# Routed experts as 79 items over sorted tokens instead of 21 chunk pairs over all tokens

## The reference, cut to what matters

```python
HID = [256, 512, 768, 1024, 256, 512, 768, 1024]
h = x @ down_w + down_b                                  # 512 -> 256
logits = x @ router_w + router_b - COST_LAMBDA * cost
probs = jax.nn.softmax(logits, axis=-1)
topv, topi = jax.lax.top_k(probs, 2)
gate = jax.nn.softmax(topv, axis=-1)
for k in range(2):
    mask = jax.nn.one_hot(topi[..., k], 8)
    acc = 0
    for e, (w1, b1, w2, b2) in enumerate(expert_params):
        hm = h * mask[..., e:e + 1]
        acc = acc + (_gelu(_gelu(hm) @ w1 + b1) @ w2 + b2)
    out = out + acc * gate[..., k:k + 1]
out = out + 0.1 * (_gelu(_gelu(h) @ shared_w1 + shared_b1) @ shared_w2 + shared_b2)
out = out @ up_w + up_b + (_gelu(x) @ core_w + core_b)
```

## Time and profile before

| | |
|---|---|
| median of 3 runs | 3310.86 us (3310.76 to 3313.55) |
| profiled execution | 3309.52 us, its span 3307.8 us |
| PE busy | 2947.3 us, 89% of the span |
| DVE, ACT, POOL busy | 62%, 46%, 7% |
| mean granted clock of PE | 0.952 |
| stage of the mixture | 617 to 1312.5 us |

### The profile page before, as it was taken

One profiled execution on the slowest core, in us unless ns is written; L12 is line 12 of the kernel. 1 busy time (PEld: TensorE's weight loads), 2 busy tenths in 40 slices (PEclk: granted clock), 3 DMA queues, 4 the chain that ended last, 5 costly groups with the idle time before them and its releaser, 6 DMA issues. The chain is left out here.

```text
span 3307.8 us, 45608 instructions
## 1 busy us (share of the span) xinstructions
PE 2947.3 (89%) x13676; PEld 1769.8 (54%) x13676; DVE 2044.3 (62%) x3875; ACT 1530.8 (46%) x3177; POOL 242.8 (7%) x234
## 2 busy tenths in 40 slices
PE   8999978799999997998998998997898888983787
PEld 4455434336999994665655655654343343432343
DVE  5566645444665665756756856754847475756776
ACT  5445422223555552444543542644555566564454
POOL 0000030002000000101102102101000000000010
PEclk9999989898999998999999999998898989895899
DMA  3000022000000001200000000001000000004000
GB/s 121 13 13 0 13 90 89 33 21 9 12 13 11 11 10 38 109 1 14 1 1 14 1 1 13 1 1 61 2 21 2 21 2 21 2 2 153 7 19 26
DMA packets 43028, 82.10 MB, mean 25 GB/s; under 512 B 6256, under 2 KB 21376, under 8 KB 39392
## 3 DMA queue, kind: packets, MB, share of 16 engines
q1 hardware_dynamic: 39952, 71.60, 6.1%
q0 software_dynamic: 2896, 8.31, 0.8%
HBM read 55.25 MB, written 4.19 MB: 18 GB/s over the span
## 5 line engine op out<-in xcount | busy, mean ns | idle before, releaser
L1765 DVE TENSOR_REDUCE x_neg_max<-bank 128x2 f32<-128x1024 f32 x256 | 299.0, 1217 | 27.8 <-PE bank L1602 27.8
L1190 PE MATMUL bank<-a_wo,a_att_cols 128*128 128x512 f32 x512 | 226.9, 594 | 6.7 <-DVE a_att_cols L1303 3.7
L1240 ACT ACTIVATE a_probs<-bank,a_neg_max 128x128 f32<-128x128 f32 (+3 forms) x256 | 138.3, 540 | 190.2 <-DVE a_neg_max L1338 189.9
L955 DVE TENSOR_TENSOR moe_hid_low<-moe_hid,moe_hid_high 128x512 fp32r<-128x512 f32 x168 | 116.3, 692 | 177.1 <-ACT moe_hid_high L825 169.8
L116 PE MATMUL bank<-all_ident,a_probs 128*128 128x128 f32 x1216 | 197.0, 275 | 17.8 <-DMA a_probs<-all_x_tok 17.8
L116 PEld LDWEIGHTS bank<-all_ident,a_probs 128*128 128x128 f32 x1216 | 155.4, 142 | 105.7 <-issue 52.5
L1232 ACT COPY a_probs_t<-bank 128x128 f32<-128x128 f32 (+3 forms) x256 | 108.6, 424 | 194.9 <-PE bank L116 194.9
L1621 PE MATMUL bank<-x_q_cols,x_k_cols 64*128 64x512 f32 x512 | 160.8, 445 | 35.7 <-ACT x_x_rows L1691 12.7
L753 PE MATMUL bank<-moe_w_high,moe_hid_low 128*128 128x256 f32 x672 | 190.3, 283 | 0.0
L753 PE MATMUL bank<-moe_w_low,moe_hid_high 128*128 128x256 f32 x672 | 190.2, 283 | 0.0
L753 PE MATMUL bank<-moe_w_high,moe_hid_high 128*128 128x256 f32 x672 | 189.4, 282 | 0.1
(11 more groups left out here) (353 smaller groups left out, 6639.0 us busy)
## 6 DMA issues: line engine op xcount, KB each, us to landing
x_x_rows<-all_x_tok SPq DMA_DIRECT2D x8, 1024.0 KB, 6.3
moe_w<-in_L_ffn_e_w SPq DMA_DIRECT2D x40, 128.0 KB, 2.2
all_x_tok<-in_x SPq DMA_DIRECT2D x1, 4096.0 KB, 17.8
x_c_rows<-in_ctx SPq DMA_DIRECT2D x8, 512.0 KB, 4.4
moe_x_rows<-all_x_tok SPq DMA_DIRECT2D x4, 1024.0 KB, 4.7
a_probs<-all_x_tok SPq DMA_DIRECT2D x4, 1024.0 KB, 4.5
a_wqkv<-in_L_attn_Wqkv SPq DMA_DIRECT2D x1, 4096.0 KB, 20.0
a_wo<-in_L_attn_Wo SPq DMA_DIRECT2D x1, 4096.0 KB, 29.6
```

The source lines that it names most:

```text
L1190: last = pe.matmul(mm[g % 2], att_cols[:, h % HALF_HEADS, j * P:(j + 1) * P], wo[:, h, :], start=h == first, stop=h == end - 1)
L1240: act.activation(probs[:, n % SLOTS, 0:t], sc[n % 4][:, 0:t], ACT.Exp, bias=neg_max[:, n:n + 1], accum_out=row_sum[:, n:n + 1]).then_inc(s ...
L1765: dve.tensor_reduce(neg_max[:, g % 2, j, 2 * pair:2 * pair + 2], pair_banks[slot % 2], AX.X, ALU.max, negate=True) \
```

## The change

The experts' weights are packed at the start: in `self_attention_0` POOL issues 60 DMAs (`pack_experts`) that copy, for each of 20 pairs of chunks, w1, w2 and b1 of the pair side by side into `packed.items`, 128 rows of 1026 values in device memory. In `cross_attention_0` POOL also clears `packed.sorted`, 6144 rows of 256 values.

In the mixture, the shared expert is computed in the first part in plain f32 (`shared_in`, `shared_out`), and gelu(h) is transposed back to rows (`turn_hidden`). The choice runs once over all 16 tiles. From it DVE computes, with one PE matmul for ranks, for each token and choice its place in an order sorted by expert, each expert's share padded to whole tiles of 256, and for each of 79 items which tile (`which[i, 0]`) and which weight pair (`which[i, 1]`) it works on. 79 is the most that any choice needs; all 79 are always run. POOL scatters gelu(h) with 32 indirect DMAs into `packed.sorted`. In the item loop SP loads tiles and weights with the numbers from `which`, PE turns a tile (`turn_rows`), multiplies in plain f32 (`hidden`, `output`), ACT copies the tile of an item and does the gelus, DVE adds the result to the tile in `acc`. Finished tiles are stored to `packed.mixed`; POOL fetches them back per token with 32 indirect DMAs, DVE weighs them (`combine`), and up projection and norm follow as before, each batch behind its rows.

```diff
+PAIRS = [c // 2 for c in CHUNKS]
+TOKENS = 256
+SPARE = (TOP_K * B * S + EXPERTS * (TOKENS - 1)) // TOKENS
+TILES = SPARE + 1
+def pack_experts(pool, packed, a):
+    for e in range(EXPERTS):
+        for n in range(PAIRS[e]):
...
+            pool.dma_start(to[:, 0:half].rearrange("p (k n) -> p k n", k=KL), chunked(a[f"L0_ffn_e{e}_w1"][:, at])) \
+                .then_inc(packed.items_in, 16)
...
+    TURN = [SPARE] + list(range(SPARE))
+    AHEAD, SLOTS, RETURNED = 4, 3, 8
...
+            def load_item(i):
+                if i >= SLOTS:
+                    sp.wait_ge(*filled(("item", i - SLOTS)))
+                pair = sp.value_load(which[i:i + 1, 1:2], min_val=0, max_val=PAIR0[EXPERTS] - 1)
+                sp.dma_start(item[:, i % SLOTS, :], packed.items[bass.ds(pair, 1)].rearrange("o p n -> p (o n)")) \
+                  .then_inc(s.item_in[i % SLOTS], 16)
+            def load_rows(n):
+                if n >= AHEAD:
+                    sp.wait_ge(*emptied(("turn", n - AHEAD)))
...
+            def store_tile(t):
+                sp.wait_ge(*emptied(("item", min((t + 1) * max(PAIRS), ITEMS) - 1)))
...
+            for i in range(SLOTS, ITEMS):
+                if i + 1 < TILES:
+                    load_rows(i + 1)
+                load_item(i)
+                if (stored + 1) * max(PAIRS) + SLOTS <= i:
+                    store_tile(stored)
+                    stored += 1
+            for t in range(stored, SPARE):
+                store_tile(t)
...
+            for n in range(AHEAD):
+                turn_rows(n)
+            hidden(0)
+            for i in range(ITEMS):
+                if i + AHEAD < TILES:
+                    turn_rows(i + AHEAD)
+                if i + 1 < ITEMS:
+                    hidden(i + 1)
+                output(i)
...
+            def take_tile(i):
...
+                tile = act.value_load(which[i:i + 1, 0:1], min_val=0, max_val=SPARE)
+                act.copy(x_now[:, i % 2, :], turned[:, bass.ds(tile, 1), :].rearrange("p o n -> p (o n)")).then_inc(s.x_now_ready, 1)
...
+            for i in range(ITEMS):
+                if i + AHEAD < TILES:
+                    keep_turned(i + AHEAD)
+                tile = dve.value_load(which[i:i + 1, 0:1], min_val=0, max_val=SPARE)
+                to = acc[:, bass.ds(tile, 1), :].rearrange("p o n -> p (o n)")
...
+                dve.tensor_tensor(to, bank(("item", i)), to, ALU.add).then_inc(free(("item", i)), 1)
...
+            fetch(0)
+            for b in range(B):
+                if b + 1 < B:
+                    fetch(b + 1)
                 layernorm_rstd(pool, st, b, m, s)
```

More of the change, by code:

```diff
@@ new lines, in mixture_of_experts, with bank, filled, room @@
+        place, fills = {}, {}
+        for ring, (first_bank, banks, at) in enumerate(((0, 2, hc_at), (2, 2, lg_at), (4, 4, mm_at))):
+            for key, n in at.items():
+                place[key], fills[key] = (first_bank + n % banks, n // banks), (s.full[ring], n + 1)
+        def bank(key):
+            return m.banks[place[key][0]]
+        def filled(key):
+            return fills[key]
+        def room(key):
+            i, use = place[key]
+            return s.free[i], use + 1
+        def emptied(key):
+            i, use = place[key]
+            return s.free[i], use + 2
@@ new lines, in core @@
+            def core(t):
+                b, j = divmod(t, NT)
+                pe.wait_ge(*emptied(("x", b, j)))
+                pe.wait_ge(*room(("core", t)))
+                for k in range(KD):
+                    last = pe.matmul(bank(("core", t)), gx[:, b, k, j * P:(j + 1) * P], w.core[:, k, :], start=k == 0, stop=k == KD - 1)
+                last.then_inc(full(("core", t)), 1)
+            for b in range(B):
+                turn_x(b)
+                if b > 0:
+                    turn_hidden(b - 1)
+                    shared_in(b - 1)
+                route_and_down(b)
+                if b > 0:
+                    shared_out(b - 1)
@@ new lines, in _ @@
+            turn_hidden(B - 1)
+            core(0)
+            core(1)
+            shared_in(B - 1)
+            pe.wait_ge(s.chosen_ready, 1)
+            pe.wait_ge(s.made, 6)
+            pe.wait_ge(*room("rank"))
+            pe.matmul(bank("rank")[:, 0:(T + 1) * EXPERTS], ones[:], counts[0][:, PAD - 1:, :].rearrange("p t e -> p (t e)"),
+                      start=True, stop=False, skip_group_check=True)
+            pe.matmul(bank("rank")[:, 0:T * EXPERTS], below[:], chosen[:].rearrange("p t e -> p (t e)"),
+                      start=False, stop=True, skip_group_check=True).then_inc(full("rank"), 1)
@@ L700, in _, with turn_gates @@
+            core(2)
+            core(3)
+            shared_out(B - 1)
+            for t in range(EARLY, T):
+                core(t)
+            pe.wait_ge(s.gate_ready, 1)
+            def turn_gates(b):
+                pe.wait_ge(*room(("gates", b)))
+                for j in range(NT):
+                    last = pe.transpose(bank(("gates", b))[0:EXPERTS, j * P:(j + 1) * P], gate[:, b * NT + j, :], m.ident[:])
+                last.then_inc(full(("gates", b)), 1)
             turn_gates(0)
@@ new lines, in hidden @@
+            def hidden(i):
+                weight = item[:, i % SLOTS, 0:KL * LATENT].rearrange("p (k n) -> p k n", k=KL)
+                pe.wait_ge(s.item_in[i % SLOTS], (i // SLOTS + 1) * 16)
+                pe.wait_ge(s.x_now_ready, i + 1)
+                pe.wait_ge(*room(("hidden", i)))
+                for c in range(2):
+                    for k in range(KL):
+                        last = pe.matmul(bank(("hidden", i))[:, c * TOKENS:(c + 1) * TOKENS], weight[:, k, c * P:(c + 1) * P],
+                                         x_now[:, i % 2, k * TOKENS:(k + 1) * TOKENS], start=k == 0, stop=k == KL - 1)
+                last.then_inc(full(("hidden", i)), 1)
@@ new lines, in output @@
+            def output(i):
+                weight = item[:, i % SLOTS, KL * LATENT:2 * KL * LATENT].rearrange("p (c n) -> p c n", c=2)
+                pe.wait_ge(*emptied(("hidden", i)))
+                pe.wait_ge(*room(("item", i)))
+                for j in range(SUB):
+                    for c in range(2):
+                        last = pe.matmul(bank(("item", i))[:, j * LATENT:(j + 1) * LATENT],
+                                         hid[:, i % 2, c * TOKENS + j * P:c * TOKENS + (j + 1) * P], weight[:, c, :],
+                                         start=c == 0, stop=c == 1)
+                last.then_inc(full(("item", i)), 1)
```

772 lines of the change are left out of this document (459 added, 313 removed).

## The result

The changed kernel takes **3397.95 us** (median of 4 runs, 3392.4 to 3400.87) against 3311.2 us for the kernel before on the same chip: 1.026 of it, with a 95% interval of 1.024 to 1.028. It is slower by 2.6%. Forecast were 3420 us with a range of 3350 to 3500. The profiled execution spans 3395.8 us, 88.0 more than the 3307.8 of before.

A forecast was written before the change was run, and what follows sets the result against it. PE work was taken to bound the loop (busy 475.7 of 476.5 us). Ahead +41.5, loop +22 and behind +46 gave +109.5 on the profiled 3309.5 us; with the median 1.3 above, 3420 us, range 3350 to 3500.

The forecast's parts named there:

- The step that decides: Loop, 19 steps (n = 5 to 23): SP's queue order delays the sorted rows, stalling PE 6.0 us (5.3 to 7.3) each.
- The size of a slow step: Loop, each of 19 steps that turn rows: 6.0 us stall plus 6.6 us work at low clock, 12.6 us (9.4 to 15).
- The fast steps: Loop, the other 60 steps: paced by the item loads at 4.25 us each (3.8 to 5.2), 255 us.
- T = (L + 3.5) / 2: Item loads in the loop: step period T, with L = 5.0 us from an output's end to the weights being there.
- the sum by that figure, 15 us lower: Loop: with a register load of about 600 ns instead of 0.9 us, the sum would be an estimated 15 us lower.
- Ahead of the loop: Mixture up to its first item: shared expert, routing and waits add 41.5 us (30 to 55), scatters hidden under 2.5 us each.
- Behind the loop: After the last item: stores, 32 fetches at 1.2 us alternating with norms, 95 us against 49.5, +46 (25 to 78).
- Elsewhere: Both attention stages: 60 packing DMAs on POOL are hidden and clearing 6 MB costs nothing, 0 us.
- A: Rival for the loop: rows come in time, all 79 steps run at 4.25 us, loop 348, total 3270 us; chance 0.07.
- B: Rival for the loop: the register load costs 2 us, loop 562, total 3485 us; chance 0.15.
- D: Rival behind the loop: indirect DMAs cost 2.2 us each, tail +32, total 3450 us; chance 0.07.
- C: Rival for the loop: item loads hide under PE, 3.7 us per step, total 3385 us; chance 0.17.

The follow-up runs named there:

- tail_tiles: Against the changed kernel, behind the loop VectorE takes tile t's fetched rows, then tile t-2's sums; GpSimd issues rstd three tiles behind a batch's last fetch: 3364.3 us, 1.016.
- rows_early: Against the changed kernel, the loads of sorted rows are put three item loads further ahead in SyncE's order: 3269.0 us, 0.988 of the kernel before.

## Why the prediction was right, and where not

**The step that decides was right.** That the rows' place in the queue takes the look-ahead away was read off the order in which SP issues, before anything ran: rows(n) behind item(n-2), which waits for `output(n-5)`. In the kernel after all 19 waits are there, and moving the rows in that order takes them away, and with them 138 us of the loop. It also carried the sign: the changed kernel lost to the one before by 87 us, and this edit alone is worth 129.

**The total of 3420 us owes something to luck.** It is 22 us above the measured 3398 because errors of both signs meet in it: the loop was put 35.5 us too high and the part behind it 3, the part ahead of it 7 us and everything else 10 too low.

**The size of a slow step was high**: 12.6 us forecast, 11.27 measured (from 857.03 to 1059.90 are 18 steps). Of 6.0 us of stall 5.2 were seen. From the end of the output to SP's issue 1.2 us were put (wake-up 0.15, register load 0.9, arithmetic 0.15) and 0.73 measured; with the address as a constant 0.02 are left, so no run shows a wake-up of 0.15, and load and arithmetic together are 0.7 and not 1.05. From the issue of the rows to PE's start on them 4.4 were put and 3.95 measured. The landing in it was put at 4.3, with 1.6 us added from the earlier trace rows; 256 KB of rows behind 513 KB took 3.7, and no run tells how much of that is the load ahead. Of 6.6 us of work 6.0 were seen: the clock's share was taken from a gap at the start of the stage. The reasoning was right in kind and 0.6 us high; a clock of about 0.6 was forecast for these steps and 0.78 was granted. 19 x 1.33 = 25 us.

**The fast steps**: T = (L + 3.5) / 2 gave 4.25, and 4.13 was measured. That wants an L of 4.8 where 5.0 was put, and one place where it can be read has it: an output ends at 1202.46 (1200.57 + 1.89), SP issues the item for its buffer at 1203.21, and PE, after a wait, starts on that item at 1207.27, 4.81 us behind the output.

```profile
1200.57 1.89 PE L929 MATMUL bank<-moe_item,moe_wide 128*128 128x256 f32 x8
...
1203.21 0.33 SPq L743 DMA_DIRECT2D moe_item<-moe_items  x1
...
1207.27 1.99 PE L919 MATMUL bank<-moe_gh_cols,moe_item 128*128 128x256 f32 x8 [1.35 <-DMA moe_item<-moe_items]
```

With 0.7 us out of L the same formula gives 3.8, and 3.75 was measured; with four buffers it gives less than PE's own time, and PE's own 3.47 was measured. What the loop has beside 19 x 11.27 is 249 us, where 255 and 4 for stores were put, 10 less. These two terms are the whole error of the loop, +22 against -13.5, and both lie within the bounds given (9.4 to 15; 3.8 to 5.2).
The Trainium skill, "DMA: Bandwidth & Descriptors", section "Latency and other measured facts", gives tensor_load a floor of about 600 ns. The trace agrees: 0.7 us here, with the arithmetic, and the sum by that figure, 15 us lower, was the nearer one.

**Ahead of the loop** +41.5 became +48.5, but for the wrong reason. The sum of the work was too high: without VectorE's waits (in tail_tiles) the part takes 199.4 us, +30, the low end of the range; which of its terms were too high, no run tells. The waits added 18.6. The step that failed is that the 32 scatters are hidden as long as one takes under 2.5 us: one took 1.27, and GpSimd was indeed done in time, but the cover was looked at only from the side of what waits for the scatters, not of what runs beside them.
Of such contention the Trainium skill, "SBUF — State Buffer", section "Who interferes with whom", says that GpSimd and VectorE exclude each other on a shared port pair, a tensor_tensor only where both its inputs are in SBUF. The add that waited has one input in a PSUM bank, and four kernels with the same add beside the same scatters have no wait; so the rule as it stands does not explain the 33.5 us, and no run here shows what does.

**Behind the loop** +46 became +42.7. The fetch was put at 1.2 us, between far bounds, and took 1.25 (0.95 and 0.30 ahead of it); the chain of norm, fetch, norm was as drawn: 20.7 us a batch and 9.8 for the last, where there is nothing more to fetch.
The Trainium skill, "SBUF — State Buffer", section "Who interferes with whom", has software DMAs starved while VectorE runs its two-port modes. The prediction priced such a hold at up to 7 us. What was seen is far smaller: a fetch that starts within the four scalings of a norm (0.5 us each) took 1.42 us in place of 0.95, twice in this stretch. That the scaling is the cause was not tried.

```profile
1343.11 1.92 DVE L97 TENSOR_SCALAR all_x_tok<-all_x_tok,moe_ln_mean_var,moe_ln_rstd 128x512 f32<-128x512 f32 x4 [1.16 <-POOL moe_ln_rstd L104]
1343.27 1.42 POOL L1280 DMA_INDIRECT moe_x_cols<-moe_mixed,moe_index  x1 [0.20 <-issue]
1344.99 0.97 POOL L1280 DMA_INDIRECT moe_x_cols<-moe_mixed,moe_index  x1 [0.30 <-issue]
```

**Elsewhere** 0 became +10. "Hidden" was said of GpSimd's 42 us of issuing, which is true (its first root still came at 125.6). What those transfers do to the DMA engines was not asked; that is the step that failed. It is worth 9 us in the kernel after (351.4 us between the roots against 342.4) and 16 in the profile of rows_early, the most of all. The clearing of 6 MB in the second stage cost nothing, as forecast.

**The rivals.** A was the right one to have: its loop was put at 348, its time at 3270, and the rows that come in time gave a loop of 324.7 and 3269.0 us (the near hit in time owes something to errors that cancel). B (a register load of 2 us) and D (an indirect DMA of 2.2) fell with 0.7 and 1.27 us. C put the fast step at 3.7; it was 4.13, nearer to the forecast, and came to 3.75 only without the register load.

## What to carry to other kernels

Buffers written ahead are no look-ahead by themselves. Take the consumer's and the issuer's order side by side, write down for each load what stands ahead of it in its queue and what that waits for, and put the load that is wanted first ahead of the one that waits for the latest event; here two lines were worth 129 us, and a chain of latency L, from the end of the last use of a buffer to its next use, tells how many buffers are needed: a step takes T = (L + work) / (buffers - 1) where that is more than the work itself. When a transfer is called hidden, ask also what it does to its neighbours, on the DMA engines and on the engines that work beside its issue: both losses that were not forecast (9 and 19 us) came beside transfers that nobody had to wait for, though how the second one comes about is open.

## What the runs showed of the hardware

- Copies from memory to memory, of rows that are 1 KB in the code, kept the 16 DMA engines at 95% and moved 96 GB/s; a 1 MB load on another queue took 23.6 us beside them and 4.8 without.
- An indirect transfer of 128 rows of 1 KB costs GpSimd 0.96 + 0.30 us for a scatter, 0.95 + 0.30 for a fetch; a plain one of the same rows 0.53.
- While such scatters ran, VectorE's adds stood still for up to 18.3 us at a time in seven of eleven profiles, and waited only for PE in four; the cause is open.
- A register load of SyncE in front of a DMA, with the arithmetic on it, costs 0.7 us.
- PE at 5.2 us of idle time in every 11.3 was granted 0.78 of the full 2.4 GHz on average, and 39 of the 138 us that the early rows gave back in the loop are that clock.
